# Four graph layers on one core: setup spread over engines, near scores by selection, maxima turned before they are split

## The reference

```python
def L0(x):   # and L2, with 4 heads of 64 columns and e_src, e_dst per head
    h = x @ W
    e = leaky_relu((h @ a1)[:, :, None] + (h @ a2)[:, None, :], 0.2)
    return elu(softmax(where(adj > 0, e, NEG)) @ h)
def L1(x):   # 8 heads of 32 columns
    q, k, v = split(x @ w_qkv)
    t = softmax(where(adj > 0, q k^T / sqrt(32), -1e9)) v
    x = layernorm(x + t) * g1 + b1
    return layernorm(x + relu(x @ w1 + bias1) @ w2 + bias2) * g2 + b2
def L3(x):
    e = leaky_relu((x @ W1) (x @ W2)^T, 0.2)
    return relu(softmax(where(adj > 0, e, NEG)) @ (x @ W3))
for L in (L0, L1, L2, L3):
    x = layernorm(x + L(x))
```

## Time and profile before

| | us |
|---|---|
| median of 3 runs | 3483.48 |
| lowest and highest | 3483.08, 3486.34 |
| the profiled execution | 3484.87 |
| its span, first to last instruction | 3482.7 |

### The profile page before, as it was taken

How to read it: one execution, slowest core, us unless ns; L and a number is a source line. 1 busy time by engine, 2 the same in 40 slices (tenths; PEclk the granted TensorE clock), 3 DMA queues, 4 the chain that set the end, 5 groups by cost and what they waited for, 6 DMA issues and landing times. The chain is left out here.

```text
span 3482.7 us, 72692 instructions
## 1 busy us (share of the span) xinstructions
PE 3151.7 (90%) x24624; PEld 1716.2 (49%) x24624; DVE 2875.7 (83%) x7804; ACT 2746.0 (79%) x5825; POOL 2074.7 (60%) x2186
## 2 busy tenths in 40 slices
PE   3898999999998999998999999999999999999866
PEld 2444445545555555455555554545455545555433
DVE  5778889888878988888988888988888888888765
ACT  1667778878878887887888887887887788888774
POOL 1345676655667555667566566655566556566564
PEclk8999999999999999999999999999999999999987
DMA  3214444445455444354444444444445444444444
GB/s 96 55 38 71 89 96 88 90 89 91 78 88 96 85 86 92 69 94 92 90 86 95 82 84 90 92 91 84 87 76 98 80 89 92 86 84 88 83 73 79
DMA packets 877891, 295.17 MB, mean 85 GB/s; under 512 B 819792, under 2 KB 856400, under 8 KB 877520
## 3 DMA queue, kind: packets, MB, share of 16 engines
q1 hardware_dynamic: 877520, 290.52, 43.9%
HBM read 21.43 MB, written 16.78 MB: 11 GB/s over the span
## 5 line engine op out<-in xcount | busy, mean ns | idle before, releaser
L763 POOL TENSOR_TENSOR split_r<-prob_r,split_r 128x512 f16<-128x512 f32 x768 | 919.8, 1209 | 1018.3 <-DVE split_r L1160 1018.3
L1123 DVE CUSTOM_DVE_ANT_0 unused<-bank_ps,neg_mask 128x512 bf16<-128x512 f32 x1024 | 664.8, 685 | 150.1 <-PE bank_ps L1308 145.7
L1374 PE MATMUL bank_ps<-val_r,trans_r 128*128 128x64 f16 (+1 forms) x9216 | 638.3, 222 | 67.0 <-DMA trans_r<-split_r 65.2
L1374 PEld LDWEIGHTS bank_ps<-val_r,trans_r 128*128 128x128 f16 x9216 | 530.3, 99 | 290.4 <-issue 101.6
L936 ACT ACTIVATE prob_r<-bank_ps 128x512 f32<-128x512 f32 x1024 | 579.3, 596 | 99.1 <-PE bank_ps L1326 95.3
L914 ACT ACTIVATE prob_r<-masked_r,low_r 128x512 f32<-128x512 f32 x768 | 553.5, 724 | 115.1 <-DVE low_r L1112 111.6
L1334 PE MATMUL bank_ps<-prob_r,value_ones 128*64 128x512 f32 (+1 forms) x2048 | 583.4, 619 | 8.9 <-ACT prob_r L936 5.2
L1160 DVE CAST split_r<-prob_r 128x512 f16<-128x512 f32 x768 | 511.7, 679 | 50.2 <-ACT prob_r L914 33.1
L1112 DVE CUSTOM_DVE_ANT_0 masked_r<-bank_ps,neg_mask 128x512 f32<-128x512 f32 x768 | 507.1, 680 | 35.8 <-ACT bank_ps L902 21.9
L902 ACT ACTIVATE bank_ps<-spread_r,near 128x512 f32<-128x512 f32 x640 | 429.1, 692 | 25.8 <-DVE low L1123 13.4
L1325 PE MATMUL bank_ps<-stack 98*128 98x512 f16 x1024 | 397.0, 388 | 27.8 <-DVE low_r L1112 14.4
(11 more groups left out here) (140 smaller groups left out, 5144.0 us busy)
## 6 DMA issues: line engine op xcount, KB each, us to landing
stack<-qk SPq DMA_DIRECT2D x384, 128.0 KB, 2.5
xcur<-in_x_dram SPq DMA_DIRECT2D x32, 512.0 KB, 3.8
out_dram<-z SPq DMA_DIRECT2D x32, 512.0 KB, 3.0
trans_r<-split_r SPq DMA_TRANSPOSE x768, 3.2
stack<-low_rows SPq DMA_DIRECT2D x128, 4.0 KB
z<-in_L_gnn_W_dram SPq DMA_DIRECT2D x4, 256.0 KB, 5.5
qk<-in_adj_dram SPq DMA_DIRECT2D x1, 1024.0 KB, 9.2
xcur<-in_L_gnn_w_qkv_dram SPq DMA_DIRECT2D x3, 256.0 KB, 3.9
```

Source lines behind the costliest of these rows:

```text
L763: nc.gpsimd.tensor_tensor(split_r[:, j, 1, :], prob_r[:, i, :], split_r[:, j, 0, :], ALU.subtract).then_inc(lo_done.sem, 1)
L1123: nc.vector.tensor_tensor_reduce(out=unused[:, nth % 2, :], in0=bank_ps[entry("bank", "sq", g, t, b, h)][:], in1=neg_mask[:, b, :], scale= ...
L1374: ins = nc.tensor.matmul(bank[:, at:at + width], trans_r[:, i, pp, jb, :], val(g, layer)[:, vp, jb, cols], start=(n == 0), stop=(n == len( ...
```

## The change

**Setup.** The loads are in seven groups with a semaphore each. SP issues the adjacency first and then the weights; ScalarE issues the vectors, columns and rows (10 loads). ScalarE scales the weights in place as they come, copies the two turned matrices, scales the product, and then makes all nine high parts in the order of `SPLIT_ORDER`; GpSimd clears `value_ones` and the parts of `stack` and makes the nine low parts. VectorE does the flags and masks, forms W a with products over all columns and a sum per head, and splits only the score weights. TensorE turns the two matrices of layer 3 first, then the flags. Work on graph 0 starts when all nine low parts, the memsets and VectorE's part are there.

**Near scores of layer 2.** The weights of `s2` get four more columns, those of the near scores; the job `c2` is gone. After `far` is written, `nr` picks the near rows, both parts, with a 0/1 matrix `sel_near`, four matmuls of 4 columns, and `nd` copies them to `near`.

**Maxima.** `mh` only scales. `mt` transposes the float32 columns to 4 rows; `mr` copies them as float16 (high), and the new `ml` on VectorE subtracts this from the bank (low). `md` waits for `ml`, and the bank stays taken until `ml`.

The diff, cut to its core:

```diff
-        2: [("s2", 0), ("c2", 0), ("h2", 0), ("h2", 1)],
+        2: [("s2", 0), ("h2", 0), ("h2", 1)],
...
+                task(("nr", g), 0.2, [("job_lo", *key)], opens=[("bank", ("nr", g))], closes=[("far", (g,))])
+                task(("nd", g), 0.14, [("nr", g)], closes=[("bank", ("nr", g))])
...
-                task(("re", *key), 0.62, [("spread", g, layer, h), ("job_lo", g, f"c{layer}", 0)], opens=[bank],
+                task(("re", *key), 0.62, [("spread", g, layer, h), ("nd", g) if layer == 2 else ("job_lo", g, "c0", 0)], opens=[bank],
...
-            task(("mh", g, t), 0.7, [("mx", g, t, b, h) for b in range(NB) for h in range(QUAD)])
-            task(("mt", g, t), 0.33, [("mh", g, t)], opens=[("bank", ("mt", g, t))])
-            task(("mr", g, t), 0.5, [("mt", g, t)] + ([("md", g - 1, t)] if g else []), closes=[("bank", ("mt", g, t))])
-            task(("md", g, t), 1.0, [("mr", g, t), ("stack", g)], lands=2.2)
+            task(("mh", g, t), 0.22, [("mx", g, t, b, h) for b in range(NB) for h in range(QUAD)])
+            task(("mt", g, t), 0.4, [("mh", g, t)], opens=[("bank", ("mt", g, t))])
+            task(("mr", g, t), 0.49, [("mt", g, t)] + ([("md", g - 1, t)] if g else []))
+            task(("ml", g, t), 0.61, [("mr", g, t)], closes=[("bank", ("mt", g, t))])
+            task(("md", g, t), 1.0, [("ml", g, t), ("stack", g)], lands=2.2)
...
+        SPLIT_ORDER = ("h0", "h2", "q", "k", "v", "f1", "f2", "h3", "g")
+        W_SPLITS = len(SPLIT_ORDER)
...
-            eng.dma_start(stage_adj, adj.rearrange("(b p) n -> p b n", p=P)).then_inc(w_loaded, 16)
+            eng.dma_start(stage_adj, adj.rearrange("(b p) n -> p b n", p=P)).then_inc(adj_loaded, 16)
+            eng.dma_start(stage_w["h0"], w_view(gat_w)).then_inc(gat_loaded, 16)
+            eng.dma_start(stage_w["h2"], w_view(mh_w)).then_inc(mh_loaded, 16)
+            eng.dma_start(stage_d1, w_view(dot_w1)).then_inc(dot_loaded, 16)
+            eng.dma_start(stage_d2, w_view(dot_w2)).then_inc(dot_loaded, 16)
+            for n, k in enumerate(("q", "k", "v")):
+                eng.dma_start(stage_w[k], w_view(w_qkv[:, n * C:(n + 1) * C])).then_inc(qkv_loaded, 16)
+            eng.dma_start(stage_w["f1"], w_view(ffn_w1)).then_inc(ffn_loaded, 16)
+            eng.dma_start(stage_w["f2"], w_view(ffn_w2)).then_inc(ffn_loaded, 16)
+            eng.dma_start(stage_w["h3"], w_view(dot_w3)).then_inc(dot_loaded, 16)
...
-                        sp.wait_ge(setup_dve, 3)
+                        sp.wait_ge(weights_lo, W_SPLITS)
+                        sp.wait_ge(setup_dve, 1)
...
+            nc.gpsimd.memset(value_ones[:], 0.0).then_inc(setup_pool, 1)
+            eng.wait_ge(setup_pool, 6)
+            nc.gpsimd.memset(stack[len(STACK) * D1:len(STACK) * D1 + 2, :, 1, :, :], 1.0 / LOW_SCALE).then_inc(setup_pool, 1)
+            eng.wait_ge(setup_pool, 7)
+            for e in range(2):
+                ones_at = 64 * e + D1
+                nc.gpsimd.memset(value_ones[:, :, :, ones_at:ones_at + 1], 1.0).then_inc(setup_pool, 1)
+            eng.wait_ge(setup_pool, 9)
+            for n, k in enumerate(SPLIT_ORDER):
+                eng.wait_ge(weights_hi, n + 1)
+                nc.gpsimd.tensor_tensor(W[k][:, 1], scaled_weight(k), W[k][:, 0], ALU.subtract).then_inc(weights_lo, 1)
...
+            eng.dma_start(stage_a0, gat_a.rearrange("(t n) o -> o t n", t=2).broadcast_to([P, 2, C])).then_inc(gat_loaded, 16)
+            eng.dma_start(stage_a2, mh_a.rearrange("(o n) -> o n", o=1).broadcast_to([P, C // 2])).then_inc(mh_loaded, 16)
...
+            eng.wait_ge(gat_loaded, 32)
+            scale_weight("h0").then_inc(weights_scaled, 1)
+            eng.wait_ge(mh_loaded, 32)
+            scale_weight("h2").then_inc(weights_scaled, 1)
+            eng.wait_ge(dots_turned, 1)
+            for half, t_tile in enumerate((stage_t1, stage_t2)):
+                nc.scalar.copy(t_tile, bank_ps[half][:].rearrange("p (t c) -> p t c", t=CT)).then_inc(dots_copied, 1)
+            eng.wait_ge(qkv_loaded, 48)
+            for k in ("q", "k", "v"):
+                scale_weight(k).then_inc(weights_scaled, 1)
+            eng.wait_ge(ffn_loaded, 80)
+            nc.scalar.activation(g1_scaled[:], g1_col[:], ACT.Copy, scale=WSCALE).then_inc(weights_scaled, 1)
+            scale_weight("f2").then_inc(weights_scaled, 1)
+            eng.wait_ge(dot_loaded, 48)
+            scale_weight("h3").then_inc(weights_scaled, 1)
+            eng.wait_ge(weights_scaled, 8)
+            for t in range(CT):
+                nc.scalar.activation(stage_f1[:, t, :], stage_w["f1"][:, t, :], ACT.Copy,
+                                     scale=g1_scaled[:, t:t + 1]).then_inc(weights_scaled, 1)
+            eng.wait_ge(gram_done, 1)
+            nc.scalar.activation(stage_g, bank_ps[0][:].rearrange("p (t c) -> p t c", t=CT), ACT.Copy,
+                                 scale=WSCALE).then_inc(weights_scaled, 1)
+            eng.wait_ge(weights_scaled, 11)
+            for k in SPLIT_ORDER:
+                nc.scalar.copy(W[k][:, 0], scaled_weight(k)).then_inc(weights_hi, 1)
...
-                        act.wait_ge(*dense_lo.at(g, f"c{layer}", 0))
+                        act.wait_ge(*(near_done.at(g) if layer == 2 else dense_lo.at(g, "c0", 0)))
...
-                    nc.scalar.copy(low_rows[:, t, :], bank_ps[entry("bank", "mt", g, t)][0:2 * QUAD, :]).then_inc(low_rows_done.sem, 1)
+                    nc.scalar.copy(low_rows[:, 0, t, :], bank_ps[entry("bank", "mt", g, t)][0:QUAD, :]).then_inc(low_rows_done.sem, 1)
...
-            eng.wait_ge(w_loaded, 16 * W_LOADS)
-            eng.wait_ge(ident_ready, 1)
+            def split_weight(dst, src):
+                after(nc.vector.tensor_copy(dst[:, 0], src))
+                after(nc.vector.tensor_tensor(dst[:, 1], src, dst[:, 0], ALU.subtract))
...
+            product = stage_scratch.rearrange("p (t n) -> p t n", t=CT)
+            for side, total in ((0, stage_near[:, :, 0]), (1, stage_s0[:, :, 0])):
+                after(nc.vector.tensor_tensor(product, stage_w["h0"], stage_a0[:, side:side + 1, :].broadcast_to([P, CT, C]),
+                                              ALU.mult))
+                after(nc.vector.tensor_reduce(total, product, mybir.AxisListType.X, ALU.add))
...
-                            after(nc.vector.tensor_tensor_reduce(
-                                out=stage_scratch[:, 0:width], in0=stage_src[:, t, h * width:(h + 1) * width], in1=a,
-                                scale=1.0, scalar=0.0, op0=ALU.mult, op1=ALU.add, accum_out=total))
...
-            for k in ("h0", "q", "k", "v", "f2", "h2", "h3"):
-                split_weight(W[k], stage_w[k], WSCALE)
-            split_weight(W["f1"], stage_f1, WSCALE)
...
+                elif kind == "nd":
+                    dve.wait_ge(*near_turned.at(g))
+                    nc.vector.tensor_copy(near[s][:], bank_ps[entry("bank", "nr", g)][:, 0:NB * HEADS[2]].rearrange(
+                        "p (b h) -> p b h", b=NB)).then_inc(near_done.sem, 1)
...
-                                                   op0=ALU.mult, op1=ALU.mult).then_inc(low_chain, 1)
-                    links += 1
-                    eng.wait_ge(low_chain, links)
-                    nc.vector.tensor_copy(low_parts[s][:, t, :, 0:QUAD], low[s][:, t]).then_inc(low_chain, 1)
-                    links += 1
-                    eng.wait_ge(low_chain, links)
-                    nc.vector.tensor_tensor(low_parts[s][:, t, :, QUAD:], low[s][:, t], low_parts[s][:, t, :, 0:QUAD],
-                                            ALU.subtract).then_inc(low_split.sem, 1)
+                                                   op0=ALU.mult, op1=ALU.mult).then_inc(low_scaled.sem, 1)
+                elif kind == "ml":
+                    t, = key
+                    dve.wait_ge(*low_rows_done.at(g, t))
+                    nc.vector.tensor_tensor(low_rows[:, 1, t, :], bank_ps[entry("bank", "mt", g, t)][0:QUAD, :],
+                                            low_rows[:, 0, t, :], ALU.subtract).then_inc(low_split.sem, 1)
...
+            eng.wait_ge(dot_loaded, 48)
...
-            eng.wait_ge(setup_dve, 2)
+            ins.then_inc(dots_turned, 1)
+            eng.wait_ge(flags_done, 1)
+            for b in range(NB):
+                nc.tensor.matmul(bank_ps[2][:, b * P:(b + 1) * P], stage_some[:, b, :], ident32[:], start=True, stop=True)
+                for kb in range(NB):
+                    ins = nc.tensor.transpose(bank_ps[4 + kb][:, b * P:(b + 1) * P], stage_flag[:, b, kb * P:(kb + 1) * P], ident32[:])
+            ins.then_inc(flags_turned, 1)
+            eng.wait_ge(dots_copied, 2)
...
+            eng.wait_ge(ffn_loaded, 80)
...
-            eng.wait_ge(setup_pool, 5)
+            ins.then_inc(gram_done, 1)
+            eng.wait_ge(setup_pool, 9)
+            eng.wait_ge(setup_dve, 1)
+            eng.wait_ge(weights_lo, W_SPLITS)
...
+                elif kind == "nr":
```

(11 more changed lines are left out.)

156 lines of the change are left out of this document (74 added, 82 removed).

## The result

The changed kernel takes 3401.8 us (median of 4 runs, 3398.0 to 3403.5), the kernel before, on the same chip, 3483.3 (3479.9 to 3486.3): a ratio of 0.9765, 95% interval 0.9748 to 0.9782. The profiled execution has a span of 3399.4 us.

What follows compares the result with a forecast made beforehand. It took TensorE's own work to bound the loop, with the setup added in full. Setup -24.7 and loop -23.5 (-21.8, +4.8, +11.5, -18) gave -48.2 us from 3483.5, so 3435, range 3410 to 3464.

Steps and rivals of the forecast that it cites:

- Part 1, the setup: Before graph 0: its first transposes start at 40.0 us instead of 64.72, a gain of 24.7 us.
- Step (a): Setup, landing of the loads: the valley in the transfer rate closes and the last weights land at 16.5 us.
- Step (b): Setup, TensorE: weight transposes about 1 us, flags' steps 4.9, products and what follows 4.9, done at 27.3 us.
- Part 2, near scores: Layer 2 in the loop: dropping `c2` saves TensorE 21.8 us, `nr` adds 4.8.
- Part 3, maxima: Maxima's turn in the loop: dearer float32 transposes +11.5 us, shorter wait before them -18, TensorE charged nothing for `ml`.
- the turn's wait, -18: TensorE's 18 waits for `low_parts` before the maxima's turn, 24.3 us, shrink by 1 us each.
- Part 4, the order: Loop from graph 0's maxima on: the planner's new order moves the time some 10 to 12 us either way.
- Only the setup: Rival: the loop keeps its time and only the setup gains, giving 3459 us; chance 0.26.
- A freer VectorE: Rival: `ml` never waits and VectorE's saved 25.7 us reach TensorE, giving 3409 us; chance 0.17.
- Slower by `ml`: Rival: `ml` stalls VectorE, every microsecond reaches TensorE, and the kernel gets slower, up to 3525 us; chance 0.04.
- the split that doesn't shorten the setup: Rival on size: last load lands at 20.5 us, GpSimd's subtractions take 1.6 each, graph 0 starts at 47: 3442.
- A rearranged order cancels all: Rival: the new order eats the gain, leaving 3480 us, within 7 us of before; chance 0.03.

Runs made afterwards that it cites:

- `setup_only`: The kernel before with only the new setup, graph loop and every engine's order unchanged: 3455.2 us, ratio 0.992.
- `near_cheap`: New setup on the kernel before, its order kept, with only 4 of the 24 matmuls of `c2` issued: 3445.4 us, ratio 0.9896.
- `turn_cheap`: New setup on the kernel before, its order kept; `mh` only scales, float32 columns turned, no low part, no `ml`: 3410.0 us, ratio 0.9793.
- `after_mh04`: The changed kernel with `mh` planned at 0.4 us instead of 0.22, order dealt anew, same instructions: 3477.4 us, ratio 0.9988.
- `before_cheap`: New setup on the kernel before, its order kept, with both `c2` cut to 4 matmuls and the turn made cheap without `ml`: 3400.4 us, ratio 0.9759.

## Why the prediction was wrong

**Part 1, the setup: right in size, by errors that cancel.** Forecast -24.7; graph 0 starts 22.3 us earlier (24.2 in `setup_only`), and the time fell by 28. Step (a), the landing, failed: 16.5 us was said, and TensorE's first transposes of the weights stand at 22.40, with the adjacency there at 8.71 as said. The valley didn't close; it only moved: the GB/s row still has one, at about 11 to 15 us, and it starts lower, with 0.5 MB in the first 5 us where the kernel before moved 0.8. ScalarE issues the small loads in that time; whether that is the reason wasn't tried. SP's issue of a late weight takes 1.75 us where the adjacency's took 0.43 before. The rule that the prediction set against itself, in the Trainium skill, DMA: Bandwidth & Descriptors, section Issuing engines are not separate DMA queues, is the one that the trace bears out: a second issuing engine brought no earlier landing (22.4 against 20.5 before). Step (b): the eight transposes take longer than said, 1.74 us, the flags' steps take 3.8 instead of 4.9, and the products are done 2.7 us after their start instead of 4.9. The granted clock is 1.00 there and was 0.57 before, which the prediction had only among its ends. They are through at 30.66; forecast 27.3. Step (d): GpSimd's nine take 10.1 us, forecast 11.3. In all 42.4 for 40.0.

**Part 2, near scores: right mechanism, too large.** Forecast -17; with the order of before 9.8 us. TensorE does 4 of 24 matmuls, but its waits of 200 to 3200 us are 186 us in `near_cheap`, whose trace lacks 288 records of matmuls, and 172 in `setup_only`: part of what a shorter job frees is waited away. `nr` takes 0.12 us where 0.15 was said.

**Part 3, maxima: the step that failed.** The term "the turn's wait, -18" was mis-sized; `turn_cheap` measures -45 for the part whose sum was -6.5. It had the wait of 24.3 us put down to `low_parts` as all that could go (ends 0 and -24). It left out that 35 of the 46 us before the turn go with the chain of VectorE, whose small instructions take over 1 us beside GpSimd and 0.18 otherwise, which their averages of 0.44 to 0.62 hide; that other waits take up two thirds of that again (the transfers of `trans_r`, +17); and, the larger term, that a third of TensorE's waits of 1 us and more are followed by a stretch at half the clock. It had no term for the clock at all; the fewer stretches are worth some 30 of the 45 us. The two values and the clock could have been read in the trace of before. The turn's +11.5 was right (0.15 us for 0.18, +10). `ml` was no risk: 0.67 us and 11.4 us of waits in 64. What remains open is how much of the 45 us is VectorE's freed time, which the prediction charged at nothing.

**Part 4, the order: the second step that failed.** "10 to 12 us either way" was worked out from the difference of stretches within one order. The order alone moves this kernel by some 75 us, or 37 either way, more than the forecast gain of the loop. The range should have been that much wider, and that the changed kernel's own order turned out a good one is luck.

**How the loop's gain adds up.** In the order of before the cheap work brings 54.8 us; the changed kernel stands 1.4 us above that, and this holds what `ml` costs and what its own order gives or takes. These two weren't separated: for `ml` by itself, and for the changed work in the order of before, there is no measurement. Nor is it known what the changed work brings in a typical order. It was timed in two, and `after_mh04` says that it can be nothing.

**The rivals.** "Only the setup" falls (53 us more). "A freer VectorE" came nearest in time (3409). In the changed kernel VectorE's busy time didn't fall, since its casts stretch. But where the order was held it did, by 54 us in `before_cheap` and 47 in `turn_cheap`, about as much as each gained, so this rival is neither shown nor refuted; against it stand only TensorE's waits for VectorE away from the turn, which didn't shrink. The 87 us of such waits that the prediction gave it were misread: the trace of before has 115.8 us in 151 waits from 200 to 3300 us. "Slower by `ml`" falls with its 11.4 us of waits. Of the split that doesn't shorten the setup the late landing came true, but the setup ended 2 us late and not 7. "A rearranged order cancels all", given 3 in 100 because it would need two bad deals of the plan, is what `after_mh04` does with one number of the plan.

## What to carry to other kernels

Where TensorE is some 90% busy, price a wait of it by more than its idle time: look at the granted clock behind it. Look at the shortest and longest of a tiny instruction and not at its mean, and shorten chains of them on the engine that feeds it. Where an order is written out by a planner, time several orders of the same work before a change of it is called a gain; here they spread over 75 us of 3400, as much as the change brought, and a new estimate for one step was worth as much as a new algorithm for it. A setup is best priced step by step from the landing of the last load, with the landing taken as late as before if the bytes are the same.

## What the runs showed of the hardware

Single waits in a loop in which TensorE is otherwise busy were followed by a granted clock of 0.50: behind one of 2.93 us, six matmuls took 2.77 us instead of 1.47. It happened behind 9 of 10 waits of over 2 us and 11 of 53 of 1 to 2 us. VectorE's casts and subtractions on 16 columns took 0.17 to 0.18 us alone and 1.07 to 1.25 us with GpSimd at work beside them. GpSimd's subtraction of 128x512 in the setup took 1.15 us, with little beside it, against 1.21 in the loop and 0.69 for VectorE's scaled subtraction of the same weights in the kernel before, 1.7 times as long. The Trainium skill, GPSIMD Engine Reference, section 3.1 Elementwise, has 1.96 times, for an addition of 2048 float32 elements. One issue of a load on SP took up to 1.75 us, at a time when no other engine issued any.
